# Last batch of a gated attention plus routed-expert kernel: one chain of work put in another order on all five queues

## The reference, cut to what matters

```python
# x: (8, 256, 512), ctx: (8, 256, 512)
def xattn(query, ctx, ...):              # 16 heads of 16, the tokens are the 512 columns
    q, k, v = Wq @ query + bq, Wk @ ctx + bk, Wv @ ctx + bv
    q, k = rotary(q), rotary(k)
    return Wm @ (softmax(q.T @ k / 4) @ v) + bm
def routed_moe(x, gate_w, w0, w1, wo):   # x: 2048 rows of 512, 8 experts, hidden size 1024
    top_logits, top_idx = top_k(x @ gate_w, 2)
    cw = scatter(softmax(top_logits))    # (2048, 8)
    for e in range(8):
        h = silu(x @ w0[e]) * (x @ w1[e])
        out += cw[:, e:e+1] * (h @ wo[e])
x = x + tanh(g_xattn) * xattn(layernorm(x), ctx)
x = x + tanh(g_ffn) * routed_moe(layernorm(x))
```

## Time and profile before

| what | value |
|---|---|
| median of 3 runs | 1112.05 us (1108.64 to 1113.96) |
| profiled execution, its own time | 1111.53 us |
| its span in the profile | 1109.7 us |
| PE busy, DVE busy, ACT busy, POOL busy | 1056.4, 805.6, 672.4, 384.5 us |
| granted clock of TensorE, mean | 0.995 of full |
| HBM read and written | 73.80 MB and 40.28 MB |

### The profile page before, as it was taken

One profiled execution on the slowest core, in us unless ns is written; L12 is line 12 of the kernel. 1 busy time (PEld: TensorE's weight loads), 2 busy tenths in 40 slices (PEclk: granted clock), 3 DMA queues, 4 the chain that ended last, 5 costly groups with the idle time before them and its releaser, 6 DMA issues. The chain is left out here.

```text
span 1109.7 us, 18854 instructions
## 1 busy us (share of the span) xinstructions
PE 1056.4 (95%) x5894; PEld 432.4 (39%) x5894; DVE 805.6 (73%) x1619; ACT 672.4 (61%) x921; POOL 384.5 (35%) x491
## 2 busy tenths in 40 slices
PE   8997999999999999988998999999999999999997
PEld 3322333333333333332343444444444444444443
DVE  7886898898889887889876766757457575755632
ACT  2276777777777777778755665746357464644421
POOL 3672745848485684612242111011101111011101
PEclk9998999999999999999999999999999999999999
DMA  6335634323235332216256775858559575864333
GB/s 205 117 93 180 203 110 174 119 87 115 90 115 138 98 98 70 99 35 219 98 164 197 176 197 138 215 122 192 130 132 226 96 204 126 223 153 74 63 57 48
DMA packets 182223, 149.65 MB, mean 135 GB/s; under 512 B 122672, under 2 KB 144176, under 8 KB 182128
## 3 DMA queue, kind: packets, MB, share of 16 engines
q1 hardware_dynamic: 170432, 126.06, 40.6%
q0 software_dynamic: 7456, 17.57, 7.9%
q10 hardware_dynamic: 4240, 4.84, 1.5%
HBM read 73.80 MB, written 40.28 MB: 103 GB/s over the span
## 5 line engine op out<-in xcount | busy, mean ns | idle before, releaser
L1501 PE MATMUL psum<-W,xs 128*128 128x512 f16 x1824 | 398.5, 380 | 4.3 <-DMA xs<-xs 2.3
L600 ACT ACTIVATE W<-psum,es 128x512 f32<-128x512 f32 x512 | 322.1, 689 | 76.6 <-PE psum L363 74.9
L844 DVE TENSOR_REDUCE MX<-psum 128x2 f32<-128x1024 f32 x256 | 310.3, 1219 | 53.3 <-PE psum L351 51.3
L1501 PEld LDWEIGHTS psum<-W,xs 128*128 128x128 f16 x1824 | 177.4, 98 | 223.9 <-issue 9.2
L363 PE MATMUL psum<-stg 50*128 50x512 f16 x512 | 142.1, 389 | 21.2 <-ACT W L600 15.1
L1775 POOL DMA_INDIRECT out<-xs,target x34 | 53.2, 1563 | 278.6 <-ACT xs L699 278.3
L1631 DVE TENSOR_TENSOR xs<-xs,psum 128x512 f32<-128x512 f32 x68 | 46.2, 685 | 129.5 <-ACT xs L684 129.3
L376 PE MATMUL psum<-W 128*32 128x512 f32 x1024 | 137.2, 608 | 0.0
L684 ACT ACTIVATE xs<-psum,i 128x512 f32<-128x512 f32 x68 | 46.2, 682 | 131.8 <-PE psum L1501 105.7
L725 DVE SCALAR_TENSOR_TENSOR W<-stg,scw,W 128x1024 f16<-128x1024 f32 x96 | 117.3, 1279 | 9.1 <-ACT W L711 9.1
L351 PE MATMUL psum<-stg 48*128 48x512 f16 x512 | 115.2, 380 | 0.2
(11 more groups left out here) (243 smaller groups left out, 1171.8 us busy)
## 6 DMA issues: line engine op xcount, KB each, us to landing
stg<-in_w SPq DMA_DIRECT2D x16, 2048.0 KB, 8.1
stg<-in_wo SPq DMA_DIRECT2D x7, 2048.0 KB
stg<-scr SPq DMA_DIRECT2D x186, 64.0 KB, 2.3
Xs<-zero SPq DMA_DIRECT2D x33, 264.0 KB, 3.3
scr<-W SPq DMA_DIRECT2D x32, 256.0 KB, 3.1
W<-W SPq DMA_DIRECT2D x60, 128.0 KB, 2.2
xs<-in_x SPq DMA_DIRECT2D x8, 512.0 KB, 3.9
out<-xs SPq DMA_DIRECT2D x8, 512.0 KB, 3.1
```

The source lines that it names most:

```text
L600: act.activation(m.Pb[:, c % 2, hh, :], m.psT[tile % 2], ACT.Exp, scale=m.es[:, hb // 2:hb // 2 + 1]).then_inc(S["exped"], 1)
L844: dve.tensor_reduce(m.MX[:, hb % 2, c0:c0 + 9:8], m.psS[tile % 2], AX_X, ALU.max, negate=True).then_inc(S["maxed"], 1)
L1501: return pe.matmul(out, rows, m.wh[(e % 2, w)][:, wp, cols], start=start, stop=stop)
```

## The change

It has eight parts, all in the stretch from about 567 to 612 us.

1. `second_gate`: PE runs 24 instead of 21 of tile 1's matmuls ahead of the transposes `job("f")`, 2 instead of 3 behind them, and 1 instead of 3 behind the router's ranks.
2. `row_sums(1, 1)` on ACT goes from behind the upper halves of expert 1's w0 to the place behind `hidden_upper(0)`.
3. `load_weights(1, 2)`, a DMA that ACT starts, goes from ahead of `result_out(0)` to behind expert 1's upper halves of w0.
4. `hold(0)`, `note(1, 0)`, `result_scale(0)`, `take_share(1)`, `undo_result(0)` and `hidden(1, 0)` on DVE go from ahead of the logits to behind `row_ends` and the last lower piece of wo.
5. `hidden(1, 1)`, the `nop` for `x_in` and `hidden_scale(1)` on DVE go from behind `plan` to ahead of it, and `hidden_lower(1)` from behind `places` to ahead of it.
6. `over_partitions(1, 1)` on POOL goes from behind the first `add` to ahead of the last batch's four scatters.
7. The notes of tile 2 are loaded by SP behind the eight zero fills instead of ahead of them.
8. The wait for these notes goes from ahead of `hidden_scale(1)` to ahead of `note(2, 0)`.

```diff
@@ tensor_attention
     job("o", NH - 2)
     job("o", NH - 1)
-    second_gate(13, 34)
+    second_gate(13, 37)
     job("f", NH - 2)
     job("f", NH - 1)
-    second_gate(34, 37)
+    second_gate(37, 39)
     job("l", NB - 1)
-    second_gate(37, 45)
+    second_gate(39, 47)
     job("r", NB - 1)
-    second_gate(45, 48)
+    second_gate(47, 48)
     first_result()
@@ scalar_attention
     hidden_upper(act, m, S, 0)
+    row_sums(act, m, S, 1, 1, m.wh[(1, 1)])
     silu(act, m, S, 1, 0, m.i0[:, 0:1], 4)
...
     row_sums(act, m, S, 1, 0, m.wh[(1, 0)])
-    load_weights(act, m, S, io, 1, 2)
     result_out(act, m, S, 0)
     hidden_upper(act, m, S, 1)
     for c in range(4):
         upper(act, m, S, 1, 0, c)
-    row_sums(act, m, S, 1, 1, m.wh[(1, 1)])
+    load_weights(act, m, S, io, 1, 2)
@@ vector_attention
     lower(dve, m, S, 0, 2, 2)
-    hold(dve, m, S, 0)
-    dve.wait_ge(S["second_notes"], 16)
-    note(dve, m, S, 1, 0)
-    result_scale(dve, m, S, 0, m.c2[:, 0:1])
-    take_share(dve, m, S, 1)
-    undo_result(dve, m, S, 0)
-    hidden(dve, m, S, 1, 0, 5)
     job("l", b)
@@ pool_attention
     rows_lower(pool, m, S, NB - 1)
     pool.wait_ge(S["rows_lower"], NB)
+    over_partitions(pool, m, S, 1, 1)
     for i in range(2):
         for k in range(2):
             scatter(NB - 1, i, k)
@@ sync_attention
     flip_hidden(sp, m, S, 0, "h_lower")
-    sp.wait_ge(S["x_noted"], 2)
-    load_notes(sp, m, slice(256, 384), slice(0, 128)).then_inc(S["rows_in"], 16)
@@ vector_experts
     dve.tensor_copy(CI[:, 17:25], CF[:, 17:25]).then_inc(S["row_ends"], 1)
     lower(dve, m, S, 0, 2, 3)
+    hidden(dve, m, S, 1, 0, 5)
+    hidden(dve, m, S, 1, 1)
+    dve.wait_ge(S["rows_in"], 16)
+    dve.nop().then_inc(S["x_in"], 3)
+    hold(dve, m, S, 0)
+    dve.wait_ge(S["second_notes"], 16)
+    note(dve, m, S, 1, 0)
+    result_scale(dve, m, S, 0, m.c2[:, 0:1])
+    take_share(dve, m, S, 1)
+    undo_result(dve, m, S, 0)
+    hidden_scale(dve, m, S, 1)
     chain(dve.tensor_tensor(NF[:, 0:8], totals, m.up, ALU.add))
...
     dve.tensor_scalar(CI[:, 25:33], NF[:, 1:9], -2.0, None, ALU.add).then_inc(S["plan"], 1)
-    hidden(dve, m, S, 1, 1)
-    dve.wait_ge(S["rows_in"], 32)
-    dve.nop().then_inc(S["x_in"], 3)
-    hidden_scale(dve, m, S, 1)
+    hidden_lower(dve, m, S, 1)
     before = NF[:, 0:8]
...
-    hidden_lower(dve, m, S, 1)
     aim(dve, m, S, 0)
     hold(dve, m, S, 1)
+    dve.wait_ge(S["rows_in"], 32)
     note(dve, m, S, 2, 0)
     scales(dve, chain, m, S, 1, 0)
@@ pool_experts
     add(0)
-    over_partitions(pool, m, S, 1, 1)
     pool.wait_ge(S["x1_last"], 16 * (NB - CUT))
@@ sync_experts
         sp.dma_start(m.Xs[bass.ds(row, n), :], m.zero[0:n, :]).then_inc(S["padded"], 16)
+    sp.wait_ge(S["x_noted"], 2)
+    load_notes(sp, m, slice(256, 384), slice(0, 128)).then_inc(S["rows_in"], 16)
     flip_hidden(sp, m, S, 1, "h_upper")
```

## The result

| | before | with the change |
|---|---|---|
| median | 1111.84 us (1108.64 to 1114.53, 10 runs) | 1115.34 us (1113.66 to 1118.71, 10 runs) |
| ratio, 95% interval | | 1.0033 (1.002 to 1.0046) |
| profiled execution: own time, span, mean granted clock | 1111.53, 1109.7, 0.995 | 1115.86, 1114.0, 0.991 |

The change costs 3.5 us (2.2 to 5.1 by the interval) where 2.5 us of gain were forecast. It is within 0.5%, but in the other direction and above the range's 1112.6.

What follows compares the result with a forecast made beforehand. PE was taken to bound the kernel, its end following the start of tile 3's gate one for one. Gate 4.3 us earlier, less 1.8 for lost clock, gave 2.5 us gained: 1109.6 us, range 1105 to 1112.6.

Steps and rivals of the forecast that it cites:

- The logits' chain: On DVE, seven instructions moved from ahead of the logits bring logits, ranks and row ends 1.38 us earlier.
- tile 2's gate: On PE, it starts directly behind `first_result`, at 588.4 us instead of 590.53.
- POOL: All-reduce at 588.6 us, scatters 0.30 behind its end, next all-reduce done at 595.3 instead of 598.74.
- Rival (d): POOL needs its other program back for the scatters, 7.0 us; the kernel slows to 1119 or 1121 us; chance 0.04.
- The first scale: On DVE, expert 1's first scale starts at 596.8 us (bounds 596.1 and 597.9), released by tile 2's notes, not POOL.
- From there to tile 3's gate: From expert 1's first scale to tile 3's gate: 10.7 us instead of 13.01, an all-reduce wait of 2.31 gone.
- The weight load: The 2 MB load of wo goes out near 601 us, lands at 609 to 614, hidden by 1.5 at the worst.
- The clock: PE idles some 3 us ahead of tile 3's gate and loses full clock inside it, costing 1.8 us.
- The sum: Tile 3's gate 4.3 us earlier, less 1.8 for the clock: 2.5 us gained; chance 0.48.
- Rival (b): First scale hardly moves or tile 3's rows come late, and the clock falls too: 1110.7 to 1112 us; chance 0.14.
- The bound for the notes: Tile 2's notes, loaded by SP, land 1.8 to 3.6 us behind their issue; 2.5 was taken.
- The slow rival that I wrote out: Same as Rival (d): POOL's program reload delays the scatters by 7.0 us, 1119 or 1121 us; chance 0.04.

Runs made afterwards that it cites:

- e7: The change with POOL's `rows_lower` of the last batch held until DVE has chosen the experts; 1115.25 us, ratio 1.0036 to before.
- e3: The change with tile 2's notes loaded behind the third of the eight zero fills; 1116.79 us, ratio 1.0028 to before.
- e2: The change with ACT's load of wo held until tile 3's rows and notes have landed; 1111.89 us, ratio 1.0004 to before.
- e1: The change with the load of wo put back ahead of `result_out(0)`, the other seven parts kept; 1113.89 us, ratio 1.0024 to before.
- e10: The kernel before with only `row_sums(1, 1)` on ACT and `over_partitions(1, 1)` on POOL moved early; 1113.32 us, ratio 1.0008 to before.
- e11: e10 with the load of wo issued from POOL's queue once tile 3's rows have landed; 1110.89 us, ratio 0.9982 to before.
- e6: The change with 20 matmuls over zeros on PE ahead of tile 3's gate; 1112.61 us, ratio 1.001 to before.
- e4: The kernel before with only the load of wo moved behind expert 1's upper halves; 1112.84 us, ratio 1.0012 to before.
- e5: The change with tile 2's notes behind the third zero fill and the load of wo held until tile 3's rows landed; 1111.59 us, ratio 0.999 to before.
- e8: e5 with nine matmuls over zeros on PE in the gap ahead of tile 3's gate; 1109.17 us, ratio 0.9983 to before.
- e9: e3 with the load of wo issued by POOL behind the first `add`, once tile 3's rows have landed; 1109.06 us, ratio 0.9967 to before.

## Why the prediction was wrong, by its own steps

**The logits' chain: right, then held by POOL.** The logits came at +12.71 (before +14.37), 1.66 earlier where 1.38 were forecast. But `rows_lower` on POOL ran to 583.94 and the cast ended at 583.97: 1.21 us instead of 0.17. Before, POOL was done at 582.21, just ahead of the cast at 582.49. Having DVE 1.4 us earlier moved it under POOL's product, which cost 1.04, so tile 2's gate came 1.40 earlier instead of 2.13. `e7` shows the cause. The Trainium skill, "SBUF — State Buffer", section "SBUF: two separate sides", says that a GpSimd instruction and certain VectorE instructions (those in a two-port mode, or with two inputs in SBUF) take a shared port pair as an exclusive lock, whose loser blocks for the whole instruction. The blocking agrees (2.13 beside 2.12); no run here shows whether the cast is such an instruction. I had read the order of each engine and not what would run beside what.

**POOL: right.** All-reduce at 589.89, +20.73, behind 5.95 us of "issue" (forecast +21.36); scatters 0.30 behind it, the next all-reduce directly behind the last scatter (595.61), with 1.02 us. Rival (d) is refuted.

**The first scale: its mechanism right, its time beyond the bound.** It was released by the notes and not by POOL, as forecast. It began at +31.32 instead of +29.56, 1.76 late, where the upper bound had been 1.1 late. The zero fills ended 0.8 later than forecast (the cast again), and DVE had the notes 3.53 us behind their issue instead of the 2.5 taken.

**From there to tile 3's gate: this step failed, through "The weight load ... hidden, by 1.5 us at the worst".** It took 13.17 us instead of 10.7, and 2.31 of that is DVE's copy waiting for tile 3's notes. I had asked only when the load's own reader would come, and there I was right: the row sums at 622.29 did not wait. I had not asked what is issued behind the load: tile 3's rows and notes, which `gate(3)` waits for. My sum had the rows near +32.3 and the load near +33.8; measured, the rows went out at +34.5, the notes at +36.8, and the load at +32.4, ahead of both. So the order was reversed from two sides. The load's side was wrong in itself: I had it go out with the end of the upper pieces, some 4 us behind the first scale, and it went out as the first of them began, 1.1 us behind the scale (before, too, it had gone out 1.1 us ahead of the end of the row sums that stand ahead of it). By my own time for the scale, 596.8, that is 597.9, or +30.7: ahead of tile 3's rows, and where `e3` (+30.4) then met the lower flip as well. `e2` shows the cost: hold the load until rows and notes are in, and from the first scale to the gate it takes 10.78 us, as forecast. Moving the load had freed the flips and put the same 2 MB on the next transfers that PE needs. The flips, the rows, the next flips: `e1`, `e3`, `e10` and `e11` each show another of them behind the load.

**The clock: right that it is lost, its price too small.** 1.8 us were forecast; the 72 matmuls took 2.66 more than the 15.71 of before, and `e6` won back 2.72. The gap was 6.27 us instead of 3, and the low stretch 6.4 us long (612.6 to 619.0) instead of 3.4. As forecast, it had cost nothing in `result(1)` before and costs in full where it is now; `e4` shows this part alone, +2.69 on the seam.

**The sum.** Forecast: gate 4.3 earlier, clock 1.8 back, 2.5 gained. Measured: gate 0.05 earlier, clock 2.66 back, 2.61 lost on the seam. The difference of 5.1 is 1.76 (first scale), 2.47 (the load) and 0.88 (clock). Rival (b) came nearest: it named late notes, late rows of tile 3 and the lost clock, but put their worst case at no change (1112). The chance of 0.81 for a time within 0.5% held, on the side that I had not expected. The bound for the notes was taken from landings on quieter queues, and none for a small transfer beside the load, though the earlier trace rows had 6.53 us for two flips beside the same load. The slow rival that I wrote out was on the wrong engine. Behind the seam nothing came back: from the seam's end to the end of the span it is 482.3 us before and 482.1 in the change, so the shift does carry to the end, as assumed.

**What stays open.** The whole run lost 3.5 us and the seam 2.6; the interval (2.2 to 5.1) holds both. The seams of `e5` and `e8` are 2.8 shorter than before's, their medians 0 and 2.4. One trace per kernel does not tell how often each execution keeps the clock. What makes the clock fall behind one gap and not behind a longer one stays open too.

## What to carry to other kernels

When a large load is moved, list what is issued after it on every queue and who waits for that, not only the load's own reader; if no place is free, tie it to the landing of the last urgent transfer, from an engine on which nobody stands behind that wait (POOL here; together with the earlier notes it took the change from 1.0033 to 0.9967 of before). Read from the trace when the load really goes out: a transfer that stands behind an engine's work in the program can leave before that work is done (4.25 us here). A gap that is removed where the next stage waits anyway comes back as a longer gap there, and that gap can cost the clock in work that everything follows. When a chain is pulled earlier, look at what each of its instructions will now run beside.

## What the hardware showed that I had not expected

- Gap length alone did not decide the clock. Lost behind 2.26 (before), 2.17 and 2.16 (`e1` and `e3`, in `e1` some 1 us into the gate; both had lost it once already at the gap before, 4.34 and 6.47), 2.10 (`e11`), 4.25, 4.60, 5.11, 5.65 and 6.27 us; kept over 1.43 (before), 1.50 and 2.36 (`e8` and `e6`, with filler ahead), 1.87 (`e9`), 2.73 (`e7`, ahead of the last 11 matmuls of `first_result`) and 3.25 us (`e5`). The Trainium skill, "TensorE: Matmul & The Clock Gate", section "Why this matters for your kernels", puts the limit at about 3 us; between 2.1 and 3.25 us these rows have both outcomes, and four losses lie well under that limit (before, `e1`, `e3`, `e11`).
- Small transfers behind the 2 MB load: 8 KB of notes took 7.05 us in the change, 7.5 in `e1` and 10.68 in `e3` (1.8 to 3.6 before); two flips took 5.51 to 7.84 us to issue (`e1`, before, `e11`, `e10`) instead of the 2.7 to 3.0 that tile 1's flips took in most other traces. The load suffers as well: 8.4 and 8.6 us where it was nearly alone (`e5`, `e2`), 10.7 and 10.9 beside tile 3's rows (the change, `e4`), 13.5, 13.9 and 16.9 beside zero fills or flips (`e1`, `e10`, `e3`).
- Some DVE instructions on two to four columns stretch to the end of a POOL product beside them: 1.21 and 2.13 us instead of 0.17. Not all do: the logits ran beside the same product in their usual 0.17 us.
- The first all-reduce behind other POOL work cost 5.77 to 6.41 us of "issue" in the traces compared here, ahead of the scatters as well as behind them, and indirect DMAs behind it only 0.30. The Trainium skill, "GPSIMD Engine Reference", section "2.1 Instruction dispatch", gives some 6 us for the first call of freshly loaded code; the size agrees, and that code is loaded there no run here shows.
